# Scores of the second block's self attention issued in two halves, the first half one step ahead; a token copy moved ahead of the second group of exponents

## The reference, cut to what matters

```
q = rope(split_heads(x @ Wq + bq))      # 16 heads of 8 features, 128 positions
k = rope(split_heads(x @ Wk + bk))
v = split_heads(x @ Wv + bv)
scores = einsum('bhqd,bhkd->bhqk', q, k) / sqrt(8)
probs  = softmax(scores)
attn   = einsum('bhqk,bhkd->bhqd', probs, v)
x = layernorm(x + attn.reshape(B, S, 128) @ Wo + bo)
```

## Time and profile before

| what | value |
|---|---|
| median of three runs | 2018.56 us (2017.13 to 2019.58) |
| the profiled execution | 2012.08 us, span 2010.4 us |
| granted TensorE clock, mean over the span | 0.987 |
| this stage (first score to last normalised row) | about 1301 to 1556 us of the span |
| PE busy in the span | 1888.9 us (94%) |
| DVE, ACT, POOL busy | 1424.3, 1214.9, 561.5 us |

### The profile page before, as it was taken

One profiled execution on the slowest core, in us unless ns is written; L12 is line 12 of the kernel. 1 busy time (PEld: TensorE's weight loads), 2 busy tenths in 40 slices (PEclk: granted clock), 3 DMA queues, 4 the chain that ended last, 5 costly groups with the idle time before them and its releaser, 6 DMA issues.

```text
span 2010.4 us, 48604 instructions
## 1 busy us (share of the span) xinstructions
PE 1888.9 (94%) x17256; PEld 1509.8 (75%) x17256; DVE 1424.3 (71%) x3597; ACT 1214.9 (60%) x3994; POOL 561.5 (28%) x894
## 2 busy tenths in 40 slices
PE   7999999999999999999899999888887788899998
PEld 6888888888888888888677777666665555767775
DVE  6678878787878787677566756578787699544443
ACT  2676767676767677787545445277776566233333
POOL 2222222222222222121122211144544477111100
PEclk9999999999999999999999999899999899899999
DMA  7100000000000000000000000300000000000000
GB/s 229 30 2 2 1 2 1 2 2 2 2 2 2 2 2 2 2 2 2 1 1 1 1 1 1 102 10 2 2 2 8 22 17 2 1 0 11 11 6 16
DMA packets 30229, 25.73 MB, mean 13 GB/s; under 512 B 5276, under 2 KB 26788, under 8 KB 29992
## 3 DMA queue, kind: packets, MB, share of 16 engines
q1 hardware_dynamic: 29992, 22.62, 3.9%
HBM read 20.52 MB, written 2.10 MB: 11 GB/s over the span
## 4 chain that ended last, share of the span: by engine, by line
issue 50%; PE 20%; POOL 15%; POOLq 9%; PEld 3%; SPq 2%; DVE 1%; DMA 1%; DVEq 0%; PEldq 0%; ACT 0%
PE bank L1317 4%; PE bank L1309 3%; POOL X L2060 3%; POOL work L1119 3%; PE bank L2187 2%; PE bank L2174 2%; PE bank L2176 2%; SPq L2460 2%; PEld bank L1317 2%; POOL work L1851 2%; POOLq L1122 2%; POOLq L1096 1%; POOL H L1123 1%; POOL X L1861 1%; POOL work L1097 1%
## 5 line engine op out<-in xcount | busy, mean ns | idle before, releaser
L782 ACT ACTIVATE work<-bank,work 128x128 f32<-128x128 f32 x1024 | 367.0, 409 | 195.6 <-DVE work L880 195.6
L551 PE MATMUL bank<-work,wbig 128*128 128x128 f32 x2048 | 261.6, 276 | 2.5 <-ACT work L845 2.5
L782 ACT ACTIVATION_READ_ACCUMULATOR work<-bank,work 128x1 f32 x1024 | 252.7, 247 | 0.0
L551 PEld LDWEIGHTS bank<-work,wbig 128*128 128x128 f32 x2048 | 245.4, 193 | 3.0 <-ACT work L845 2.7
L887 DVE TENSOR_TENSOR work<-work 128x512 f32<-128x512 f32 x256 | 178.9, 699 | 20.1 <-issue 1.3
L797 ACT ACTIVATE work<-bank 128x512 f32<-128x512 f32 x256 | 173.6, 678 | 27.7 <-PE bank L564 27.7
L880 DVE TENSOR_REDUCE work<-bank 128x4 f32<-128x512 f32 x256 | 159.1, 686 | 33.5 <-PE bank L590 33.5
L564 PE MATMUL bank<-ident,work 128*128 128x128 f32 x1024 | 158.2, 277 | 17.9 <-DVE work L887 17.7
L564 PEld LDWEIGHTS bank<-ident,work 128*128 128x128 f32 x1024 | 113.9, 141 | 66.6 <-issue 40.5
L1383 ACT ACTIVATE work<-bank,col_b 128x512 f32<-128x512 f32 x128 | 87.7, 691 | 108.4 <-PE bank L1309 108.2
L2348 DVE TENSOR_TENSOR work<-wff,bank 128x320 f32<-128x320 f32 (+1 forms) x128 | 62.5, 489 | 124.3 <-ACT wff L2263 123.8
(11 more groups left out here) (343 smaller groups left out, 4101.6 us busy)
## 6 DMA issues: line engine op xcount, KB each, us to landing
wbig<-in_moe_w SPq DMA_DIRECT2D x2, 1536.0 KB, 9.4
work<-in_mask_l SPq DMA_DIRECT2D x8, 256.0 KB, 2.8
out<-X SPq DMA_DIRECT2D x8, 256.0 KB, 2.3
H<-in_moe_w SPq DMA_DIRECT2D x3, 512.0 KB, 8.6
wff<-in_moe_w SPq DMA_DIRECT2D x1, 1024.0 KB
X<-in_x SPq DMA_DIRECT2D x1, 512.0 KB, 4.2
wbig<-in_sa_wq SPq DMA_DIRECT2D x1, 512.0 KB, 3.7
wbig<-in_sa_wk SPq DMA_DIRECT2D x1, 512.0 KB, 4.5
```

The source lines that it names most:

```text
L551: last = nc.tensor.matmul(o[:, j * T:(j + 1) * T], w[:, t * 128:(t + 1) * 128], src, start=True, stop=True)
L782: last = nc.scalar.activation(at_probs[:, g, h, :], bank[g][:, h * T:(h + 1) * T], ACT.Exp, bias=at_nmax[:, g, h:h + 1], accum_out=at_den[ ...
```

## The change

Three edits in one. PE issues the scores of a sequence as two halves of two matmuls each (banks 0 and 1, then banks 2 and 3); the first half of sequence t+1 goes into step t between turn(t,1) and turn(t,2), and each half waits only for the exponents of its own two banks. DVE follows: greatest(t+1,0) moves into step t, between heads(t-1) and turned(t). ACT copies the tokens out of bank 7 right behind exps(t,0), no longer behind exps(t,1).

The order after it:

- PE: score(t, second half), turn(t-1,3), output(t-1), project(t+2), tokens(t), turn(t,0), weigh(t-1), turn(t,1), score(t+1, first half), turn(t,2)
- ACT: turned(t-1,3), exps(t,0), tokens(t), exps(t,1), turned(t,0), exps(t,2), exps(t,3), turned(t,1)
- DVE: greatest(t,1), values(t), residual(t-2), greatest(t,2), greatest(t,3), stats_(t-2), rope(t+2), heads(t-1), greatest(t+1,0), turned(t)

```diff
-            def score(b):
+            def score(b, second):
                 pe.wait_ge(l1.kblk, b + 1)
-                need(pe, l1.probs, QUAD * b)
-                for i in range(QUAD):
+                if b >= 1:
+                    pe.wait_ge(l1.probs, QUAD * (b - 1) + 2 * second + 2)
+                for i in range(2 * second, 2 * second + 2):
...
             for t in range(-3, B + 2):
                 now = 0 <= t < B
-                if now:
-                    score(t)
+                if t == 0:
+                    score(0, 0)
+                if now:
+                    score(t, 1)
...
                 if now:
                     turn(t, 1)
+                    if t + 1 < B:
+                        score(t + 1, 0)
                     turn(t, 2)
...
                 if now:
                     exps(t, 0)
-                    exps(t, 1)
                 if t + 3 < B:
                     tokens(t)
                 if now:
+                    exps(t, 1)
                     turned(t, 0)
...
             def greatest(b, g):
-                dve.wait_ge(l1.scores, b + 1)
+                dve.wait_ge(l1.scores, 2 * b + g // 2 + 1)
...
-                if now:
-                    greatest(t, 0)
+                if t == 0:
+                    greatest(0, 0)
+                if now:
                     greatest(t, 1)
...
                     heads(t - 1)
+                if 0 <= t + 1 < B and now:
+                    greatest(t + 1, 0)
                 if now:
                     turned(t)
...
-                need(pool, l1.scores, b - 1)
+                need(pool, l1.scores, 2 * (b - 1))
```

## The result

The changed kernel takes 2027.37 us (median of 6 runs, 2023.58 to 2029.09) against 2019.11 us (6 runs, 2017.13 to 2019.58): ratio 1.0041, interval 1.0028 to 1.0054. It is slower, as forecast; 2031.8 was predicted, 2021 to 2040 as range. The steady step went from 7.73 to 8.13 us where 8.09 was predicted.

The account below looks back on a forecast made before the run. No engine is full, so a chain across engines sets the 7.73 us step. Steady steps 10.1, steps 29 and 30 1.9 and the start 1.2 make 13.2 us; on 2018.56 that gives 2031.8 us, range 2021 to 2040.

Parts of the forecast that it names:

- The token copy: Ahead of weigh on PE: the 0.78 us wait is for ACT's copy, and moving the copy earlier removes all of it.
- The side sum for a whole score: Steady step had the old score stayed whole: PE would need 6.94 us, ACT slightly more.
- The price of a half: Score on PE: a half of two matmuls costs 1.07 us, the same as the whole score.
- The first rival: Score on PE: a half costs only 0.53 us, step 7.03 us, total 1998.8 us; chance 0.08.
- The change of shape: PE between transposes and score: each change costs about 0.08 us, so four transposes followed by a score half take 0.55.
- Steps 29 and 30: Late steps without a token copy: nothing gained, 7.14 us before and 8.09 after, 1.9 us for both.
- The start: Start of the stage, both halves back to back: between 0 if merged and 2 us, taken as 1.2 us.
- The sum: Whole kernel: 10.1 + 1.9 + 1.2 = 13.2 us slower, added to the median alike, 2031.8 us.
- The second rival: Ahead of turn(t,0): the wait for group 0's exponents shrinks, step 7.75 us, total 2020.4 us; chance 0.10.
- The third: Rival at weigh: it waits for something else, the token move gains nothing, step 8.87 us, 2053.6 us; chance 0.06.
- the fourth: Rival at the score: a half's passes run one after another, 1.92 us a half, 2083 us; chance 0.03.
- The signs: Expected in the timeline: two score rows a step, weigh 0.6 behind turn(t,0), step 8.1 us, ACT and DVE idle up 0.4.

Follow-up runs that it names:

- e3: Kernel before with only ACT's token copy moved behind the exponents of group 0, scores whole; 2004.45 us, ratio 0.9931, step 7.33 us.
- e4: Changed kernel with ACT's order of the kernel before, so only the scores are split; 2049.03 us, ratio 1.0153, step 8.90 us.
- e5: Changed kernel with scores in three packs (bank 0, bank 1, banks 2 and 3) parted by other work; one run, 2061.47 us, step 9.18 us.
- e2: Changed kernel without any edit, measured and profiled once more; ratio 1.0051 (1.0031 to 1.0071), step 8.13 us.
- e6: Changed kernel with both halves issued back to back in the old place, both behind all four exponent groups; one run, 2027.48 us, step 7.90 us.

## Why the prediction was right

- **The token copy.** The wait of 0.78 us ahead of weigh was ACT's copy: shown by e3 and e4. The side sum for a whole score gave 6.94 from PE and "slightly more" from ACT; it is 7.33, so "slightly" was 0.4. The prediction had the numbers for it: exps(t,3) done at 6.10, 0.14 to the score, 1.07 for the score make 7.31.
- **The price of a half.** 1.07 predicted, 1.06 measured, by the argument from the earlier trace rows: a matmul's two passes follow one another, and idle row quarters shorten neither. e5 shows it for one matmul alone. Why a pass on row tiles takes 0.53 us where one on the full array takes 0.43 isn't shown; the prediction took the 0.53 as it stood. The first rival (0.53) falls in the slivers above. The rule of the Trainium skill (TensorE: Matmul & The Clock Gate, Measured speedup vs the span model) agrees: a few ns per row tile, here 0.02 us from one tile to four.
- **The change of shape.** 0.55 predicted from four transposes to the score behind them, 0.59 and 0.58 measured (1406.68 to 1407.27, 1408.33 to 1408.91). That is most of what the step lies above 8.09: 2.37 + 0.59 + 1.88 + 0.59 + 1.06 + 0.58 + 1.06 = 8.13. The Trainium skill (TensorEngine Tiling, Key Properties) says that a change of tiling mode drains the engine. By the prediction's estimate a full drain at each would have made the step 8.33 (8.09 and 0.24); the trace doesn't show that much.
- **Steps 29 and 30.** 7.15 before, 8.13 after: 1.97 us, 1.9 predicted.
- **The start.** 1.2 us predicted, 0.36 measured (first score to first turn of group 3, 9.01 and 9.37 us). This term was mis-sized: two halves without work between them are one pack, 2.02 us as before. I had left the merging open. The early half of sequence 1 falls in this stretch too, mostly in time in which PE stood still before (1.03 us ahead of turn(0,2), 0.47 ahead of the next score). With the halves alone (e4) the stretch takes 8.94 us, so they cost nothing here; the 0.36 shows only with the token copy moved as well.
- **The sum.** In the stage 28 x 0.401 + 1.97 + 0.36 = 13.6 us, 13.2 predicted. That it came so close is in part luck: the steps cost 11.2 where 10.1 was predicted, the start 0.36 where 1.2 was. Of the 13.6, 8.3 us showed in the medians and 10.3 by e2's ratio, so 2031.8 lies 4.4 us above the 2027.37 measured. What did not hold is "the change adds to the median alike": the old kernel's executions had the low mean clock more often than the changed kernel's. Sorted by clock, the change costs 14 us or more.
- **The second rival** (the wait for group 0's exponents vanishes) fell: turn(t,0) still comes 2.37 us behind turn(t-1,3). The third and the fourth fell with e3 and the slivers.
- **The signs.** ACT's idle time grew by 0.5 us a step and DVE's by 0.3, 0.4 predicted for both. The others came as written: two rows a step of four passes each in two slivers of two, weigh 0.6 behind turn(t,0), the wait ahead of turn(t,0), a step of 8.1.

## What to carry to other kernels

Float32 matmuls on separate row tiles cost one pack here, 1.05 to 1.07 us for one, two or four of them; issue them together, and count a whole pack more for each part that is moved apart by other work. Moving all four early wasn't tried. A wait that is removed pays only up to the next chain: the same copy was worth 0.40 us a step with the whole score and 0.77 with the halves. Before a change of a few tenths of a per cent is judged by medians, sort the executions by granted clock, and read the step length in the trace, which repeated within 0.02 us for both kernels.

## What was not expected of the hardware

- The passes of one pack are taken across calls: in the changed kernel's first score all four first passes start within 20 ns, then all four second passes, though two calls with a wait and an increment each issued them. In e6, where both calls wait for the same last exponents, the second call's passes start 0.12 us later and still lie beside the first call's.
- The mean granted clock of one kernel's executions falls into groups (0.987 to 0.989 and 0.980 to 0.983 for the kernel before), some 9 us apart in time, more than the 8.3 us by which the medians of the two kernels differ.
